# Cross-attention on one core: the scores of two slots formed together, in six PSUM banks

## Chip, core and metric

One NeuronCore of a Trainium2 chip runs the whole kernel in one launch. The metric is device time in microseconds (us). Below, PE is TensorE (matmuls), DVE is VectorE, ACT is ScalarE, POOL is GpSimd and SP is the queue that issues most DMAs. PSUM has eight banks of 512 fp32 per partition; matmuls write there, and SBUF is the working memory.

## What is computed

```python
a = layer_norm(audio_kv, gamma, beta)                      # 32 x 375 x 512
Q = heads(x @ Wq.T); K = heads(a @ Wk.T); V = heads(a @ Wv.T)   # 16 heads of 32
scores = einsum('bhtd,bhsd->bhts', Q, K) / sqrt(32)        # 112 queries x 375 keys
attn = softmax(where(mask, scores, -inf))
out = (attn @ V) @ Wo.T
return x + tanh(gate) * out                                # 32 x 112 x 512, all fp32
```

The large products are taken in three passes of a split (high part times high part, high times low, low times high), so one product over 512 inputs is 12 matmuls.

## The kernel before

The batch of 32 is cut into 128 **slots**: a slot is one batch with one group of four heads, so a batch has four. Keys run in three chunks of 125. The layer norm is folded in: the scores are made from raw context, and each chunk is scaled by the rows' `rstd` when ACT evicts it.

A slot `n` goes through these steps, each on one engine, handed on by semaphores:

- PE projects K (`project_k`, product at L874, bank `KB`), ACT copies it to `kT` (L654).
- PE forms the scores (`scores`, L1023): 12 matmuls of 32 rows, four heads on the four 32-row strips of the array, into the four banks of `sbank` (24 instructions in the trace). ACT evicts three chunks of 125x448 (`scores_out`, L574) into `prob`, which has four slots (`NB`).
- DVE takes maxima in each quadrant of 32 (`quadrant_maxima`, L780). SP stores them to DRAM and loads them back in another order (`exchange_maxima`, L332, L339). DVE reduces them (`row_maximum`, L767) and spreads them to 128x448 by a transpose (L770) into `spread`.
- DVE subtracts `spread` from the three chunks (`subtract_maximum`, L790); ACT takes the exponentials (L635).
- POOL adds the three chunks (`sum_chunks`, L451 and L455); PE forms the weighted sums (L1042) and the denominators (L1054) for two slots at a time in bank `PB`; ACT copies them out (L613).

Once per batch, PE projects V three times and the output once (L874, bank `VO`), ACT evicts them (L663, L590), DVE takes row statistics (L704, L707), normalises (`normalise`, L795 to L805, which uses `spread` for the denominators) and forms the low half of the split (`low_half`, L809). POOL finishes `rstd` (`row_statistics`, L393 to L402), makes the low half of the context (`context_lo`, L424, once per slot), adds the bias to x (`add_bias`, L436) and the output (`result`, L442).

The order on each engine is written out by hand, unrolled: the function `slot` of each engine lists what it does in slot `n`, most of it for slots `n-1` (evictions), `n-3` (subtraction, exponential) and `n-4` (weighted sums). PE, in a pair of slots, has: K, V, [weighted sums of two slots], scores, K, V or output, scores. The eight banks are: four for scores, `KB` = 4, `VO` = 5, `MB` = 6, `PB` = 7. `spread` lies in PSUM:

```python
KB, VO, MB, PB = 4, (5, 5), 6, 7
spread = bank[MB][:, 0:HT]
```

Of the kernel before, what the change touches and what calls it, by code (L numbers as in the profile page):

```python
# [5 lines left out]
F32 = mybir.dt.float32  # L6
# [8 lines left out]
KT = D // 128  # L15
# [7 lines left out]
LOOP = 2 * KT  # L23
# [10 lines left out]
def xattn(nc, xT, x, ctx, ctxT, mask, wqT, wkT, wvT, woT, gamma, beta, gate, out, row_max):  # L34
    es = ExitStack()
    with es:
# [54 lines left out]
        def cut_f(name):  # L91
# [35 lines left out]
        rden = sb("rden", [128, BLK])  # L127

        sbank = es.enter_context(nc.psum_tensor("sbank", [128, HC, 512], F32))
        bank = [sbank[:, h, :] for h in range(HC)] + [  # L130
            es.enter_context(nc.psum_tensor(f"bank{i}", [128, 512], F32))[:, :] for i in range(4, 8)]
# [5 lines left out]
        mean_bank = {"k": bank[3], "v": bank[7]}  # L137
        bv_bank, bo_bank = bank[6][:, 0:KT], bank[7]
# [52 lines left out]
        s_mm = sem("s_mm")  # L191
        s_out = sem("s_out")
# [25 lines left out]
        passed = sem("passed")  # L218
# [9 lines left out]
        def live(i, k, shift, count):  # L228
            return not isinstance(i, int) or 0 <= k * i + shift < count

        def behind(i, k, shift):
            return not isinstance(i, int) or k * i + shift > 0

        def first_two(i, c):
            return isinstance(i, int) and 2 * i + c < 2

        def wait_apart(engine, s, value):
            engine.wait_ge(s, value)
            if not isinstance(value, int):
                engine.sem_inc(passed)  # L240

        def slots(engine, slot, first=-1, last=SLOTS // LOOP + 2):
            for i in range(first, last):
                for r in range(LOOP):
                    slot(i, r)

        def v_item(r):
            b, u = r // KT, r % KT
            return {3: (b + 1, 0), 0: (b, 1), 1: (b, 2), 2: (b, None)}[u]

        def late_v(i, c, j):

            return isinstance(i, int) and 2 * i + c == B - 1 and j > 0

        def is_slot(i, r, n):
            return isinstance(i, int) and LOOP * i + r == n

        def weighted(n):

            if n >= SLOTS - 1:  # L260
                return [n - 3] if n - 3 < SLOTS else []
            return [n - 4, n - 3] if n % 2 == 0 and n >= KT else []

        def whole(i, c):

            return live(i, 2, c, B) and not (isinstance(i, int) and 2 * i + c == B - 1)
# [4 lines left out]
        def load_ctx(queue, i, m):  # L271

            if behind(i, LOOP, m - 2 * KT + 1):
                wait_apart(queue, c_done, i * LOOP + (m - 2 * KT + 1))
            queue.dma_start(cn[:, m % (2 * KT), :], ctxT_v[i * 2 + m // KT, :, m % KT, :]) \
                .then_inc(ld_ctx[m % (2 * KT)], 16)

        def load_rows(queue, i, c):
            if behind(i, 2, c):
                wait_apart(queue, stats_done, i * 2 + c)  # L280
            for part in (slice(0, 120), slice(120, SP_)):
                queue.dma_start(rows[part, :, :], rows_v[i * 2 + c, part, :, :]).then_inc(ld_rows, 16)

        @block.sync
        def _(sync):
            def load_xT(i, g):
                sync.dma_start(xraw[:, g, :, :], xT_v[:, :, bass.ds(i * (2 * GN) + g * GN, GN)]) \
                    .then_inc(ld_xT[g], 16)
# [4 lines left out]
            def load_x(i, c):  # L293
                sync.dma_start(xy[0:T, c % 2, :], x[i * 2 + c, :, :]).then_inc(ld_x[c % 2], 16)
# [6 lines left out]
            load_xT(0, 1)  # L301
            load_rows(sync, 0, 0)
            load_w("k", raw_k)
            sync.wait_ge(xr_done, 1)
            load_xT(1, 0)
            load_w("v", raw_v)
            sync.wait_ge(xr_done, 2)
            load_xT(1, 1)
            load_w("o", raw_o)
            load_rows(sync, 0, 1)  # L310
            for m in range(KT):
                load_ctx(sync, 0, m)
            for n in range(4, GROUPS):
                sync.wait_ge(xr_done, n - 1)
                load_xT(n // 2, n % 2)
            sync.dma_start(mask_u8[0:B, :], mask).then_inc(ld_mask, 16)
            load_rows(sync, 0, 2)
            for m in range(KT, 2 * KT):
                load_ctx(sync, 0, m)
            sync.wait_ge(mean_mm["v"], 1)  # L320
            load_x(0, 0)
            sync.wait_ge(bv_mm, 1)
            load_x(0, 1)

            def exchange_maxima(i, r):

                p = LOOP * i + r - 1
# [3 lines left out]
                sync.wait_ge(quad_max, i * LOOP + r)  # L331
# [4 lines left out]
                wait_apart(sync, max_stored, i * (16 * LOOP) + r * 16)  # L336
# [6 lines left out]
            def slot(i, r):  # L343
                c, u = divmod(r, KT)
                if live(i, LOOP, r - 1, SLOTS):
                    exchange_maxima(i, r)
                if u == 0:
                    if live(i, 2, c - 3, B):
                        wait_apart(sync, y_done, i * 2 + (c - 2))
                        sync.dma_start(out[i * 2 + (c - 3), :, :], xy[0:T, (c - 3) % 2, :]) \  # L350
                            .then_inc(stored[(c - 3) % 2], 16)
                if u == 1 and live(i, 2, c - 1, B) and not first_two(i, c - 1):
                    wait_apart(sync, stored[(c - 1) % 2], i * 16 + (c - 1) // 2 * 16)
                    load_x(i, c - 1)
            slots(sync, slot)
# [4 lines left out]
        def _(pool):  # L360
# [22 lines left out]
            def then(ins):  # L383
                ins.then_inc(ln_step, 1)
                steps[0] = steps[0] + 1
                wait_apart(pool, ln_step, steps[0])

            def row_statistics(i, c):

                P = SP_  # L390
                steps[0] = i * (2 * STEPS) + c * STEPS
                wait_apart(pool, stats_done, i * 2 + (c + 1))
# [5 lines left out]
                if not first_two(i, c):  # L398

                    wait_apart(pool, s_out, i * (LOOP * ST) + (c - 1) * KT * ST)  # L400
                    wait_apart(pool, v_done, i * (2 * ST) + (c - 1) * ST)
# [16 lines left out]
            def context_lo(i, r, ahead):  # L418
                if not live(i, LOOP, r + ahead, SLOTS):
                    return  # L420
                m = r + ahead
                p, k = m // KT % 2, m % KT
                wait_apart(pool, c_hi, i * LOOP + (m + 1 - KT))
# [4 lines left out]
            def wait_x(i, c):  # L428
                if c % 2:
                    wait_apart(pool, ld_x[1], (i + (c + 1) // 2) * 16)  # L430
                else:
                    wait_apart(pool, ld_x[0], (i + c // 2 + 1) * 16)

            def add_bias(i, c):
                wait_x(i, c)
# [3 lines left out]
            def result(i, c):  # L439
                wait_apart(pool, xb_done, i * 2 + (c + 1))  # L440
                wait_apart(pool, y_out, i * 2 + (c + 1))
# [3 lines left out]
            def sum_chunks(i, r):  # L445

                q, h = (r - 3) % NB, (r - 3) % 2
                wait_apart(pool, exp_done, i * (LOOP * ST) + ((r - 3) * ST + 2))
                if behind(i, LOOP, r - 4):
                    wait_apart(pool, pv_mm, i * LOOP + (r - 4))  # L450
                pool.tensor_tensor(psum[0:SP_, h, :], prob[0:SP_, q, 0, :], prob[0:SP_, q, 1, :],  # L451
                                   ALU.add).then_inc(sum_half, 1)
                wait_apart(pool, sum_half, i * LOOP + (r - 2))
                wait_apart(pool, exp_done, i * (LOOP * ST) + ((r - 3) * ST + 3))
# [3 lines left out]
            def slot(i, r):  # L458
                c, u = divmod(r, KT)
                if is_slot(i, r, 0):  # L460
                    mask_bias()
                if behind(i, LOOP, r + 2):
                    context_lo(i, r, 5)
                if u == 1 and live(i, 2, c + 1, B) and not first_two(i, c + 1):
                    row_statistics(i, c + 1)
                if live(i, LOOP, r - 3, SLOTS - 3):
                    sum_chunks(i, r)
                if u == 0 and whole(i, c - 2):
                    add_bias(i, c - 2)
                if is_slot(i, r, SLOTS + 3):  # L470
                    add_bias(i, c - 1)
                if u == 3 and whole(i, c - 2):
                    result(i, c - 2)
# [4 lines left out]
            row_statistics(0, 0)  # L478
# [5 lines left out]
            row_statistics(0, 1)  # L484
# [14 lines left out]
            slots(pool, slot)  # L499

        @block.scalar
        def _(act):
# [14 lines left out]
            def q_group(n):  # L517
                for m in range(KT):
                    act.wait_ge(q_mm, n * KT + m + 1)
                    act.activation(qT[:, n * GB:n * GB + GB, m, :], bank[KT * (n % 2) + m][:, 0:GN]  # L520
                                   .rearrange("p (b t) -> p b t", t=T), ACT.Copy).then_inc(q_out, 1)

            def context_hi(i, r):
                m = r + 6
                c, k = divmod(m, KT)
                act.wait_ge(ld_ctx[m % (2 * KT)], (i + m // (2 * KT) + 1) * 16)
# [601 lines left out]
```

## Time and profile before

| | |
|---|---|
| three runs | 977.51, 980.29, 980.42 us; median 980.29 us |
| profiled execution | span 975.2 us from the first to the last instruction; its own time outside the span is not on the page, so the median stands 5.1 us above the span |
| granted PE clock, mean | 0.998 |
| busy | PE 98%, PE weight loads 83%, DVE 82%, ACT 71%, POOL 60% of the span |

The first 95 us or so project Q and prepare the weights; the last 25 us or so finish the last slots. Between lies a stretch that repeats every batch. [...]

### The profile page before, as it was taken

Reading aid. Unit: us, or ns where it says so; the run is one execution under the profiler, and the core shown is the slowest. Engines: PE = TensorE matmul, PEld = TensorE weight load, DVE = VectorE, ACT = ScalarE, POOL = GpSimd, SP = SyncE. Lnnn points to the kernel's source line nnn. Section 1 sums busy time; section 2 is a strip of 40 time slices with the busy share of each in tenths; the row PEclk is TensorE's granted clock in tenths of the full one; section 3 lists DMA queues with packets and bytes.
Section 4 is the critical chain, followed back from the end, with each engine's and each line's share of the span. In section 5 each row is a group of like instructions: output and inputs, shape, how many; then the busy total and the mean of one; then the engine's idle time right before and its main releaser. Section 6 shows DMA issues by size and latency. Waiting matters only on the chain.

```text
span 975.2 us, 26736 instructions
## 1 busy us (share of the span) xinstructions
PE 954.5 (98%) x10703; PEld 805.6 (83%) x10703; DVE 795.5 (82%) x1446; ACT 694.3 (71%) x1301; POOL 588.6 (60%) x661
## 2 busy tenths in 40 slices
PE   8999999999999999999999999999999999999976
PEld 7889878888888888888888888888888888888864
DVE  6962588888888888888988888888888888888786
ACT  2422677778777787777877777777778777787773
POOL 0851356676666666666767666666676666666641
PEclk9999999999999999999999999999999999999999
DMA  9750333433333343333333333343332334331111
GB/s 280 224 148 24 74 82 79 101 90 80 85 88 94 87 101 94 98 98 92 87 79 86 99 88 94 93 100 99 96 93 72 83 96 95 87 100 39 34 38 48
DMA packets 80093, 90.89 MB, mean 93 GB/s; under 512 B 21888, under 2 KB 58752, under 8 KB 79968
## 3 DMA queue, kind: packets, MB, share of 16 engines
q10 hardware_dynamic: 29311, 46.24, 19.4%
q1 hardware_dynamic: 50657, 42.93, 16.5%
q8 instruction: 85, 1.39, 0.6%
q14 instruction: 40, 0.33, 0.1%
HBM read 79.05 MB, written 10.09 MB: 91 GB/s over the span
## 4 chain that ended last, share of the span: by engine, by line
PE 91%; DMA 3%; DVE 2%; POOL 2%; ACT 1%; issue 0%; SPq 0%; ACTq 0%; DVEq 0%; POOLq 0%
PE bank L874 64%; PE sbank L1023 11%; PE bank L1042 8%; PE bank L897 3%; PE bank L1054 2%; PE sbank L897 2%; DMA qT<-in_wvT 1%; ACT shared_f L574 1%; POOL gbo L411 1%; DVE shared_f L790 1%; POOL xy L415 1%; DMA row_stats<-rmax 1%; ACT shared_f L635 0%; DMA qT<-in_wqT 0%; POOL shared_f L451 0%
## 5 line engine op out<-in xcount | busy, mean ns | idle before, releaser
L574 ACT ACTIVATE shared_f<-sbank,maskT,rstd 125x448 f32<-125x448 f32 x384 | 250.5, 722 | 128.0 <-PE sbank L1023 128.0
L451 POOL TENSOR_TENSOR shared_f<-shared_f 125x448 f32<-125x448 f32 x125 | 146.9, 1175 | 276.7 <-ACT shared_f L635 276.7
L874 PE MATMUL bank<-shared_r,w_k 128*128 128x376 f32 x1536 | 298.0, 343 | 1.2 <-ACT shared_f L654 1.2
L780 DVE TRANSPOSE_TENSOR_REDUCE rmax<-shared_f 128x14 f32<-128x448 f32 x384 | 220.5, 620 | 89.3 <-ACT shared_f L574 82.5
L874 PE MATMUL bank<-w_v,shared_r 128*125 128x512 f32 x1152 | 284.9, 396 | 0.0
L874 PEld LDWEIGHTS bank<-shared_r,w_k 128*128 128x128 f32 x1536 | 258.2, 188 | 14.9 <-ACT shared_f L654 1.4
L874 PEld LDWEIGHTS bank<-w_v,shared_r 128*125 128x125 f32 x1152 | 213.5, 186 | 45.5
L790 DVE TENSOR_TENSOR shared_f<-shared_f,bank 125x448 f32<-125x448 f32 x384 | 215.4, 616 | 4.4
L635 ACT ACTIVATE shared_f<-shared_f 125x448 f32<-125x448 f32 x384 | 198.0, 579 | 6.6 <-DVE shared_f L790 6.6
L455 POOL TENSOR_TENSOR shared_f<-shared_f 125x448 f32<-125x448 f32 x125 | 143.6, 1149 | 9.8
L1023 PEld LDWEIGHTS sbank<-qT,shared_f 32*125 32x125 f32 x3072 | 95.3, 183 | 36.9 <-issue 36.9
L1023 PE MATMUL sbank<-qT,shared_f 32*125 32x112 f32 x3072 | 118.1, 282 | 2.2 <-ACT shared_f L574 2.2
L424 POOL TENSOR_TENSOR shared_r<-cn,shared_r 128x375 fp32r<-128x375 f32 x124 | 114.1, 921 | 9.6 <-ACT shared_r L530 9.5
L1042 PEld LDWEIGHTS bank<-shared_f 125*32 125x32 f32 x3072 | 71.3, 110 | 30.4 <-issue 24.4
L1042 PE MATMUL bank<-shared_f 125*32 125x112 f32 x3072 | 87.7, 261 | 5.4 <-ACT shared_f L613 3.4
L663 ACT ACTIVATE shared_f<-bank,rstd 125x512 f32<-125x512 f32 x94 | 64.6, 687 | 39.7 <-PE bank L874 39.7
L874 PE MATMUL bank<-w_o,shared_r 128*112 128x512 f32 x372 | 91.6, 394 | 0.1
L770 DVE STREAM_TRANSPOSE bank<-top 128x448 f32<-128x448 f32 x128 | 84.4, 660 | 4.4
L874 PEld LDWEIGHTS bank<-w_o,shared_r 128*112 128x112 f32 x372 | 64.5, 174 | 18.3 <-DVE shared_r L809 0.3
L654 ACT ACTIVATE shared_f<-bank 128x376 f32<-128x376 f32 x128 | 61.9, 484 | 8.6 <-issue 5.5
L530 ACT ACTIVATE shared_r<-cn 128x375 fp32r<-128x375 f32 x124 | 64.8, 523 | 0.3 <-issue 0.3
L704 DVE BATCH_NORM_STATS2 stats<-rows 125x6 f32<-125x512 f32 x96 | 58.9, 667 | 0.8 <-DMA rows<-in_ctx 0.8
(95 smaller groups left out, 775.9 us busy)
## 6 DMA issues: line engine op xcount, KB each, us to landing
cn<-in_ctxT ACTq DMA_DIRECT2D x120, 187.5 KB, 2.5
rows<-in_ctx ACTq DMA_DIRECT2D x29, 720.0 KB
xy<-in_x SPq DMA_DIRECT2D x32, 224.0 KB, 3.4
out<-xy SPq DMA_DIRECT2D x32, 224.0 KB, 3.6
shared_f<-in_xT SPq DMA_DIRECT2D x7, 896.0 KB, 9.2
x<-row_stats SPq DMA_DIRECT2D x64, 84.0 KB
x_odd<-row_stats SPq DMA_DIRECT2D x64, 84.0 KB
row_stats<-rmax SPq DMA_DIRECT2D x128, 21.0 KB
```

The source lines that it names most:

```text
L424: pool.tensor_tensor(cT[:, p, 1, k, 0:S], cn[:, m % (2 * KT), :], cT[:, p, 0, k, 0:S].bitcast(F32), ALU.subtract) \
L451: pool.tensor_tensor(psum[0:SP_, h, :], prob[0:SP_, q, 0, :], prob[0:SP_, q, 1, :], ALU.add).then_inc(sum_half, 1)
L455: pool.tensor_tensor(psum[0:SP_, h, :], psum[0:SP_, h, :], prob[0:SP_, q, 2, :], ALU.add).then_inc(sum_done, 1)
L530: act.activation(cT[:, c % 2, 0, k, 0:S], cn[:, m % (2 * KT), :], ACT.Copy) \
L574: act.activation(prob[0:SP_, (r - 1) % NB, j, :].rearrange("p (h t) -> p h t", h=HC), sbank[0:SP_, :, T * j:T * j + T], ACT.Identity, bias ...
L635: act.activation(prob[0:SP_, (r - 3) % NB, j, :], prob[0:SP_, (r - 3) % NB, j, :], ACT.Exp, scale=SCALE).then_inc(exp_done, 1)
L770: dve.transpose(spread.rearrange("p (k a) -> p k a", a=32), top[:, :].unsqueeze(2).to_broadcast([128, BLK, 32])) \
L780: last = dve.tensor_reduce(rmax[:, (r - 1) % 2, BLK * j:BLK * j + BLK], prob[:, (r - 1) % NB, j, :].rearrange("p (k a) -> p k a", a=32), A ...
L790: dve.tensor_tensor(prob[0:SP_, (r - 3) % NB, j, :], prob[0:SP_, (r - 3) % NB, j, :], spread[0:SP_, :], ALU.subtract).then_inc(sub_done, 1)
L874: last = pe.matmul(dst, l, m, start=(start and k == 0), stop=(stop and k == len(pairs) - 1))
L1023: last = pe.matmul(bank[h][0:SP_, T * j:T * j + T], kT[part, r % 2, SP_ * j:SP_ * j + SP_], qT[part, 2 * i + c, u, :], start=True, stop=True)
L1042: pe.matmul(bank[PB][HD * h:HD * h + HD, p % 2 * T:p % 2 * T + T], v_sb[0:SP_, c % 2, j, col:col + HD], prob[0:SP_, p % NB, j, T * h:T * h ...
```

## The change

PE, ACT, DVE, POOL and SP are written for pairs of slots (64 of them). PE does K of slot 2m, V, K of slot 2m+1, V or output, the weighted sums of the pair before the last, and then the scores of both slots in one stretch. The scores of two slots (six chunks of four heads) take six banks, two of which hold a third chunk each. The weighted sums go to the bank of K. `spread` gets a tensor in SBUF. ACT evicts the six chunks, one K, then takes the exponential of slot 2m-1; the exponential of slot 2m comes at the end of its pair.

```diff
-        KB, VO, MB, PB = 4, (5, 5), 6, 7
-        spread = bank[MB][:, 0:HT]
-        late_bank = {1: bank[VO[0]], 2: bank[KB]}
+        spread = sb("spread", [128, HT])
+        psum_all = es.enter_context(nc.psum_tensor("banks", [128, 8, 512], F32))
+        bank = [psum_all[:, i, :] for i in range(8)]
+        KB, VO = 6, 7
...
+        def score_place(n, j):
+            r = 3 * (n % 2) + j
+            if r < 2:
+                return (0, 1, 2, 3), (r, r, r, r)
+            if r < 4:
+                return (0, 1, 4, 5), (r, r, r - 2, r - 2)
+            return (2, 3, 4, 5), (r - 2, r - 2, r - 2, r - 2)
...
 (PE)
+            def scores(n):
+                c, u = divmod(n, KT)
+                pe.wait_ge(k_done, n + 1)
+                if n % 2 == 0:
+                    need(pe, s_out, n * ST)
                 for j in range(ST):
+                    banks, places = score_place(n, j)
+                    if n % 2 and j == 1:
+                        pe.wait_ge(s_row, n // 2 + 1)
                     for h in range(HC):
...
+                    if n % 2 == 0 and j == 1:
+                        last.then_inc(s_row, 1)
+                if n % 2:
+                    last.then_inc(s_mm, 1)
...
+            def slot_pair(m):
+                c, odd = divmod(m, 2)
+                project_k(2 * m)
+                if not odd:
+                    project_v(c, 0)
+                elif c < B - 1:
+                    project_v(c, 2)
...
+                project_k(2 * m + 1)
+                if not odd and c < B - 1:
+                    project_v(c, 1)
+                if odd and 2 <= c < B - 1:
+                    output(c - 2, c * ST + ST)
+                if pair(m - 2):
+                    pe.wait_ge(k_done, 2 * m + 2)
+                    weighted_sums(2 * m - 4, bank[KB])
...
+                scores(2 * m)
+                scores(2 * m + 1)
...
 (ACT)
+            def slot_pair(m):
+                c, odd = divmod(m, 2)
+                if pair(m):
+                    second_out(m)
+                if pair(m - 2):
+                    weighted_out(2 * m - 4)
+                if pair(m):
+                    scores_out(2 * m)
+                    scores_out(2 * m + 1)
+                if pair(m + 1):
+                    k_out(2 * m + 2)
+                if pair(m - 1):
+                    exponential(2 * m - 1)
...
+                if pair(m + 1):
+                    first_out(m + 1)
...
+                for n in (2 * m + 6, 2 * m + 7):
+                    if n < SLOTS:
+                        context_hi(n)
+                if pair(m + 1):
+                    k_out(2 * m + 3)
+                    if odd and whole(c - 1):
+                        high_half(c - 1)
+                if pair(m) and m < PAIRS - 1:
+                    exponential(2 * m)
...
 (DVE)
+            def slot_pair(m):
+                c, odd = divmod(m, 2)
+                if pair(m - 1):
+                    row_maximum(2 * m - 1)
+                    subtract_maximum(2 * m - 1)
+                if not odd and whole(c - 2):
+                    low_half(c - 2)
+                quadrant_maxima(2 * m)
+                quadrant_maxima(2 * m + 1)
+                if not odd and 2 <= c + 2 < B:
+                    statistics(c + 2)
+                if odd and whole(c - 1):
+                    normalise(c - 1)
+                if m < PAIRS - 1:
+                    row_maximum(2 * m)
+                    subtract_maximum(2 * m)
...
 (POOL)
+            def slot_pair(m):
+                c, odd = divmod(m, 2)
...
+                if pair(m - 1):
+                    sum_chunks(2 * m - 2)
+                    sum_chunks(2 * m - 1)
+                if not odd and m >= 0:
+                    if c + 1 < B and c > 0:
+                        row_statistics(c + 1)
+                    if whole(c - 2):
+                        add_bias(c - 2)
+                if odd and whole(c - 2):
+                    result(c - 2)
+                for n in (2 * m + 6, 2 * m + 7):
+                    if n < SLOTS:
+                        context_lo(n)
...
 (SP)
+            for m in range(PAIRS):
+                c, odd = divmod(m, 2)
+                exchange_maxima(2 * m)
+                exchange_maxima(2 * m + 1)
+                if not odd and c > 2:
+                    store(c - 3)
+                if odd and c > 2:
+                    load_x(c - 1)
```

The instructions of the subtraction, the reductions, the exponentials and the sums keep their shapes. Banks used while the kernel starts and while it ends are renumbered, and the end takes its last four slots as one pair and two single ones.

## Rows read from the trace of the kernel before

**Rows 1.** Page, busy time of each engine (busy us, share, instructions).
```profile
PE 954.5 (98%) x10703; PEld 805.6 (83%) x10703; DVE 795.5 (82%) x1446; ACT 694.3 (71%) x1301; POOL 588.6 (60%) x661
```

**Rows 2.** Page, the chain that ended last, share of the span by engine.
```profile
PE 91%; DMA 3%; DVE 2%; POOL 2%; ACT 1%; issue 0%; SPq 0%; ACTq 0%; DVEq 0%; POOLq 0%
```

**Rows 3.** Windows: one batch; length, busy time and instructions by engine.
```profile
500.00:526.96 26.96, 26.96 (x321) 22.69 (x320) 23.07 (x44) 20.82 (x39) 17.56 (x21) 1.00 0.38 92
```

**Rows 4.** Timeline of PE: start, duration, line, output and inputs, count.
```profile
502.56 2.33 PE L874 MATMUL bank<-shared_r,w_k 128*128 128x376 f32 x12
504.73 2.95 PE L874 MATMUL bank<-w_v,shared_r 128*125 128x512 f32 x12
...
506.58 1.10 PE L874 MATMUL bank<-w_v,shared_r 128*125 128x512 f32 x4
507.61 0.92 PE L1023 MATMUL sbank<-qT,shared_f 32*125 32x112 f32 x24
508.14 0.40 PE L1023 MATMUL sbank<-qT,shared_f 32*125 32x112 f32 x8
508.25 0.29 PE L1023 MATMUL sbank<-qT,shared_f 32*125 32x112 f32 x4
508.46 0.44 PE L874 MATMUL bank<-shared_r,w_k 128*128 128x376 f32 x1
...
513.51 1.36 PE L1042 MATMUL bank<-shared_f 125*32 125x112 f32 x48
...
526.99 1.36 PE L1042 MATMUL bank<-shared_f 125*32 125x112 f32 x48
```

**Rows 5.** Page, costliest groups: the K projections (busy, mean ns of one).
```profile
L874 PE MATMUL bank<-shared_r,w_k 128*128 128x376 f32 x1536 | 298.0, 343 | 1.2 <-ACT shared_f L654 1.2
```

**Rows 6.** By line: DVE's two-input instructions, ns min/median/max, first and last start.
```profile
L790 DVE TENSOR_TENSOR shared_f<-shared_f,bank x384: 611/614/623, 112.6 to 964.9; 125x448 f32<-125x448 f32 x192
...
L805 DVE TENSOR_TENSOR shared_f<-shared_f,bank x31: 620/620/622, 144.4 to 950.5; 128x448 f32<-128x448 f32 x31
...
L809 DVE TENSOR_TENSOR shared_r<-shared_f,shared_r x31: 624/1514/1536, 149.3 to 956.6; 128x448 fp32r<-128x448 f32 x31
```

**Rows 7.** Timeline of DVE in the same batch.
```profile
499.62 1.52 DVE L809 TENSOR_TENSOR shared_r<-shared_f,shared_r 128x448 fp32r<-128x448 f32 x1
...
502.23 1.68 DVE L790 TENSOR_TENSOR shared_f<-shared_f,bank 125x448 f32<-125x448 f32 x3
503.83 1.69 DVE L780 TRANSPOSE_TENSOR_REDUCE rmax<-shared_f 128x14 f32<-128x448 f32 x3
```

**Rows 8.** Timeline of POOL in the same batch.
```profile
499.51 1.15 POOL L455 TENSOR_TENSOR shared_f<-shared_f 125x448 f32<-125x448 f32 x1
500.62 1.66 POOL L436 TENSOR_TENSOR xy<-xy,gbo 112x512 f32<-112x512 f32 x1
...
508.01 0.98 POOL L424 TENSOR_TENSOR shared_r<-cn,shared_r 128x375 fp32r<-128x375 f32 x1
...
521.49 1.29 POOL L442 TENSOR_TENSOR xy<-xy,gated 112x512 f32<-112x512 f32 x1
```

**Rows 9.** Timeline while weights are prepared: DVE and POOL side by side.
```profile
46.11 0.69 DVE L713 TENSOR_TENSOR w_v<-qT,w_v 128x512 fp32r<-128x512 f32 x1
47.74 2.39 DVE L713 TENSOR_TENSOR w_v<-qT,w_v 128x512 fp32r<-128x512 f32 x2
...
44.59 3.57 POOL L411 TENSOR_SCALAR gbo<-qT,bv 128x512 f32<-128x512 f32 x1
48.23 1.34 POOL L415 TENSOR_TENSOR gated<-gated,gbo 128x512 f32<-128x512 f32 x1
```

**Rows 10.** Timeline of ACT: three score evictions, one of K.
```profile
502.70 1.96 ACT L574 ACTIVATE shared_f<-sbank,maskT,rstd 125x448 f32<-125x448 f32 x3 [1.87 <-PE sbank L1023]
...
506.37 0.49 ACT L654 ACTIVATE shared_f<-bank 128x376 f32<-128x376 f32 x1
```

**Rows 11.** Waits: who waited for whom, us in total, times, longest.
```profile
POOL shared_f L451 <- ACT shared_f L635: 276.7, 123, 5.5
```

More of the change, by code:

```diff
@@ L226, in xattn @@
         wT = {"k": wkT, "v": wvT, "o": woT}
[L228 to L266, printed above, removed]
+        def need(engine, s, value):
+            if value > 0:
+                engine.wait_ge(s, value)
+        def q_bank(g, m):
+            return bank[KT + (m + 2) % KT] if g else bank[m]
+        def score_place(n, j):
[5 more added lines that the diff above has]
+            return (2, 3, 4, 5), (r - 2, r - 2, r - 2, r - 2)
@@ L341, in exchange_maxima @@
                     ap=[[0, HC], [HC * ST * BLK, 32], [1, HC * ST * BLK]])).then_inc(ld_max[q], 16)
[L343 to L355, printed above, removed]
+            for m in range(PAIRS):
[6 more added lines that the diff above has]
+                    load_x(c - 1)
+            for b in range(B - 3, B):
+                store(b)
+                if b + 2 < B:
+                    load_x(b + 2)
             sync.wait_ge(stored[0], 16 * (B // 2))
@@ L456, in sum_chunks @@
                                    ALU.add).then_inc(sum_done, 1)
-            def slot(i, r):
-                c, u = divmod(r, KT)
-                if is_slot(i, r, 0):
+            def slot_pair(m):
+                c, odd = divmod(m, 2)
+                if m == 0:
                     mask_bias()
[L462 to L473, printed above, removed]
+                if pair(m - 1):
[11 more added lines that the diff above has]
+                        context_lo(n)
@@ L498, in _ @@
             pool.wait_ge(c_done, KT)
-            slots(pool, slot)
+            for m in range(-1, PAIRS):
+                slot_pair(m)
+            add_bias(B - 2)
+            result(B - 2)
+            add_bias(B - 1)
         @block.scalar
@@ new lines, in scores, with weighted @@
+                        last = pe.matmul(bank[banks[h]][0:SP_, T * places[h]:T * places[h] + T],
+                                         kT[part, n % 2, SP_ * j:SP_ * j + SP_],
+                                         qT[part, c, u, :], start=True, stop=True)
+                    if n % 2 == 0 and j == 1:
+                        last.then_inc(s_row, 1)
+                if n % 2:
+                    last.then_inc(s_mm, 1)
+            def weighted(p, j, dst):
+                c, u = divmod(p, KT)
+                for h in range(HC):
+                    col = HD * (HC * u + h)
+                    pe.matmul(dst[HD * h:HD * h + HD, :], v_sb[0:SP_, c % 2, j, col:col + HD],
+                              prob[0:SP_, p % NB, j, T * h:T * h + T],
+                              start=(j == 0), stop=(j == ST - 1))
```

560 lines of the change are left out of this document (249 added, 311 removed).

## Prediction

> **What bounds the kernel now.** I read the busy times first, then the chain, then one batch of the repeating stretch. PE is busy 98% of the span, DVE 82%, POOL 60% [rows 1]; the chain that ended last runs through PE for 91% [rows 2]. In the batch from 500.00 to 526.96 PE is busy 26.96 of 26.96 us, DVE 23.07, ACT 20.82, POOL 17.56 [rows 3]. So in that stretch every other engine is hidden, DVE with the least room: 3.9 us a batch. PE's timeline gives the period of a pair of slots: 526.99 - 513.51 = 13.48 us [rows 4]. The same timeline shows what going into and out of the scores costs, and the lines of DVE and POOL show what DVE's room depends on.
>
> **What PE saves.** Of two score stretches per pair one disappears as a stretch of its own. Going in: V's matmuls start every 0.231 us ((506.58 - 504.73) / 8), but from the fourth last to the first score it is 1.03 us, where four take 0.93: 0.10 us. The stretch: 508.46 - 507.61 = 0.85 us for six groups of four matmuls that follow each other at 508.25 - 508.14 = 0.11 us, so 0.66 would do: 0.19 us. Going out: the first K matmul lasts 0.44 us where the mean is 0.343: 0.10 us [rows 4, 5]. Together 0.39, say 0.40 us a pair, and over 64 pairs 25.6 us. PE's period would be 13.08 us a pair, 26.16 a batch.
>
> **Waits added on PE.** The odd slot's second chunk waits for the even slot's second chunk (`s_row`). Behind it stand the last eight score matmuls, then K. Two chunks, four groups at 0.11 us, lie between, 0.44 us against the 0.29 us of a group [rows 4]: I take 0. If the wait emptied the array each time, it would cost what leaving and entering costs, 0.40 us a pair, and the whole saving; a gain is excluded, since nothing is removed. The second K waits for the K copy behind six evictions: PE has a K and a V to do first, 507.61 - 502.56 = 5.05 us; ACT needs 0.14 us to start (502.70 after 502.56), twice 1.96, and 0.49: 4.55 us [rows 4, 10]. Hidden, with 0.5 us of room; if ACT comes to the evictions more than that late, PE stands, and with it the V and the weighted sums queued behind. The weighted sums share the bank of K; ACT copies them out while PE forms the scores, and PE's K waits behind that copy. The first slot's scores are evicted only when both are formed, up to 0.85 us later; DVE's reductions start later by that, with nothing added to DVE's own work. Renumbered banks at start and end, and stores and loads moved between SP's two exchanges of a pair: I take 0; SP's exchange for a second slot queues behind the first, and DVE has statistics or a normalisation to do meanwhile. Shapes of evictions and exponentials stay; six banks instead of four give the same 448 columns, so 0, either way by less than the 0.5 us of room.
>
> **What the new place of `spread` costs.** This is the term that decides. Today the subtraction reads `prob` from SBUF and `spread` from PSUM: 384 of them take 611 to 623 ns, whatever POOL does, and so does the normalising product (620 to 622). The low half, of the same 448 columns but with both inputs in SBUF, takes 624 ns at the least and 1514 in the median [rows 6]. One instance shows why: it starts at 499.62 while POOL's sum runs from 499.51 to 500.66, and ends at 501.14; had it run its 0.624 us undisturbed at the end, it began at 500.52, when POOL was nearly done. POOL's next instruction starts at 500.62 and takes 1.66 us, but ends 1.14 us after DVE's [rows 7, 8]. So the two engines take turns: a two-input DVE instruction from SBUF and a POOL addition do not run together. After the change all 12 subtractions of a batch and the normalising product are of that kind, besides the low half: 14 instead of 1.
>
> Without any of these waits DVE needs 23.07 - 0.89 = 22.2 us a batch [rows 3, 6]. PE's new period is 26.16. So DVE can wait 4.0 us a batch, 0.28 us for each of the 14, before it becomes the bound, and 4.8 us, 0.34 each, before the change loses to the old period; and that is if it never idles for anything else.
>
> How many waits are there? The order of the new program says which POOL instructions are ready when. POOL's idle time is nearly all waiting for exponentials (276.7 us before its first sum) [rows 11], so its work comes in bunches behind them. In a pair, ACT's exponential of slot 2m-1 comes after the six evictions and a K, about when DVE finishes the reductions. POOL then adds that slot's chunks (two instructions of 1.15 us) while DVE does statistics or normalises, some 2 us. When DVE comes to the subtractions of slot 2m, POOL has three instructions queued: the bias (1.14) or the result (1.29), and two context halves (0.85 to 0.98) [rows 8]. If the engines alternate, three subtractions meet three of them: 0.9 + 0.85 + 0.85 = 2.6 us. The subtractions of slot 2m+1 follow at once, and POOL's sums of slot 2m, whose exponentials have just been taken, run beside them: one whole wait of about 1.0 and part of another, 1.4 us together. That is 4.0 us a pair, 8.0 a batch, 0.67 us for each of the 12. The lower bound is 0 (POOL always elsewhere; a gain is excluded, as 614 ns in PSUM stands against 624 in SBUF at the least). The upper is the low half's 0.89 for all 14, 12.5 us. I take 8.0, nearer to the low half, the only row of this kind in this stretch.
>
> DVE then needs 22.2 + 8.0 = 30.2 us a batch, 3.24 over today's 26.96. Over 31 batches (the first and last are incomplete) that is +100 us. PE's 25.6 us are not to be had, since PE waits for DVE by way of ACT: late subtractions delay the exponential, the evictions behind it, and the K copy. The span goes from 975.2 to 1075.6; with the 5.1 us by which the median of the runs stands above the span, 1080.7, say **1080 us**.
>
> The start of the kernel shows the same turns, and an exception [rows 9]. Two back-to-back two-input instructions from 47.74 take 2.39 us, where one undisturbed takes 0.69: POOL's addition, begun at 48.23 during the first, came in between them. But at 46.11 such an instruction ran in 0.69 us although a POOL instruction had stood since 44.59 behind the DVE instruction before it: DVE passed it.
> [...]
>
> **Rivals.**
> 1. *DVE keeps its turn through three subtractions.* Then each group waits at most once. Four groups at about 0.6 us on average (POOL is busy 17.56 of 26.96 us [rows 3], a wait is at most 0.9), and 0.5 each for product and low half: 3.4 us, so DVE needs 25.6 us, below 26.16. PE stays the bound and keeps its saving: 980.3 - 25.6 = 955 us, up to 970 if some waits reach PE. For it: the row at 46.11. Against it: 47.74, and that POOL's L455 and L436, issued back to back, let the low half in between [rows 8, 9]. Faster; chance 0.21.
> 2. *Full waits everywhere.* 22.2 + 12.5 = 34.7 us, +7.7 a batch, +240: 1220 us. For it: the low half's median is near its maximum [rows 6]. Against it: POOL would need 14 large instructions lined up with 14 of DVE's, and as the period grows POOL idles more. From 1150 on: chance 0.08.
> 3. *Waits that nearly cancel the saving.* About 4.8 us of DVE waits a batch, or the `s_row` wait emptying the array each time at 0.40 us a pair, gives back the 25.6: 977 to 983 us. Chance 0.06.
> 4. *Milder turns*: 5 to 6 us a batch, up to 983 to 1020 us: the random meeting of the two engines rather than bunches. Chance 0.09.
>
> **How the numbers follow.** Forecast 1080, own range 1020 to 1150, chance 0.56. About 0.3% (3 us) is what a measurement of this kernel tells from no change. Slower: 0.56 + 0.08 + 0.09 = 0.73; same 0.06; faster 0.21. Cases of both signs lie far apart; the range from 956 to 1150 takes in most of the first rival, and leaves out its lowest part and the second.
>
> **What would show it.** Right: L790 of 384 instructions at a mean of about 1.2 to 1.3 us instead of 0.615, the normalising product above 0.62; DVE busy above 95% of the repeating stretch, PE well under 90%, with its idle time before K, released by ACT's K copy; a batch of about 30 us. PE's own saving still visible: 12 groups of scores in one stretch of about 1.5 us. Wrong: subtractions near 0.62 to 0.8 us and a batch near 26.2 us (first rival); subtractions undisturbed and PE idle before the odd slot's second chunk (`s_row`); or DVE idle while PE waits, by the maxima exchange through DRAM, which I left out of the sum.

## The result: 24% slower

The changed kernel takes 1214.18 us in the median of 4 runs (1209.93 to 1218.74), against 978.9 us of the kernel before in the same comparison: a ratio of 1.2407, 95% interval 1.237 to 1.2444. The direction was forecast, the size was not: 1080 us, with a range that ended at 1150.

The page of the kernel after, busy times and the chain that ended last by engine and by line, answers to [rows 1, 2]; its line numbers have moved by a few.

```profile
PE 1005.3 (83%) x10687; PEld 873.3 (72%) x10687; DVE 835.7 (69%) x1446; ACT 694.1 (57%) x1299; POOL 602.6 (50%) x663
...
DMA 59%; DVE 24%; issue 7%; PE 5%; SPq 3%; POOL 1%; ACT 0%; ACTq 0%; DVEq 0%; POOLq 0%
DMA row_stats<-rmax 39%; DMA x_odd<-row_stats 17%; DVE shared_f L793 9%; DVE rmax L783 7%; PE banks L905 4%; DVE spread L774 4%; SPq L335 3%; DVE top L771 3%; DMA x<-row_stats 1%; DMA qT<-in_wvT 1%; PE banks L882 1%; POOL gbo L406 1%; POOL xy L410 0%; DVE shared_r L812 0%; DMA qT<-in_wqT 0%
```

No engine is near full. The chain has left PE and lies in two small DMAs, the store and the load of the maxima. One batch, from one block of weighted sums to the one two pairs on, as a window (length, then busy time by engine), answers to [rows 3]: 34.13 us instead of 26.96.

```profile
601.18:635.31 34.13, 27.80 (x321) 24.22 (x320) 23.64 (x43) 20.85 (x39) 17.92 (x21) 0.95 0.27 73
```

DVE's busy time in this batch grew by only 0.6 us, to 23.64; over the run it grew by 40.2 us (795.5 to 835.7), 1.3 a batch. Forecast were 30.2 us a batch. DVE waits instead. Its timeline in one pair (idle time before an instruction and what ended it stand in brackets):

```profile
608.34 3.27 DVE L783 TRANSPOSE_TENSOR_REDUCE rmax<-shared_f 128x14 f32<-128x448 f32 x6
...
613.12 0.81 DVE L808 TENSOR_TENSOR shared_f<-shared_f,spread 128x448 f32<-128x448 f32 x1
619.29 0.43 DVE L771 TENSOR_REDUCE top<-x 128x14 f32<-128x168 f32 x1 [5.36 <-DMA x<-row_stats]
619.76 0.65 DVE L774 STREAM_TRANSPOSE spread<-top 128x448 f32<-128x448 f32 x1
620.44 1.70 DVE L793 TENSOR_TENSOR shared_f<-shared_f,spread 125x448 f32<-125x448 f32 x3
623.10 0.44 DVE L771 TENSOR_REDUCE top<-x_odd 128x14 f32<-128x168 f32 x1 [0.97 <-DMA x_odd<-row_stats]
623.58 0.65 DVE L774 STREAM_TRANSPOSE spread<-top 128x448 f32<-128x448 f32 x1
624.26 1.95 DVE L793 TENSOR_TENSOR shared_f<-shared_f,spread 125x448 f32<-125x448 f32 x3
...
626.67 3.27 DVE L783 TRANSPOSE_TENSOR_REDUCE rmax<-shared_f 128x14 f32<-128x448 f32 x6
```

The same time on SP's queue, issue of store (L328) and load (L335); a load is issued when its store has landed (by the waits, L335 stood for the stores 128 times, 416.0 us in all):

```profile
610.11 0.52 SPq L328 DMA_DIRECT2D row_stats<-rmax  x1
615.72 0.54 SPq L335 DMA_DIRECT2D x<-row_stats  x1
616.35 0.53 SPq L328 DMA_DIRECT2D row_stats<-rmax  x1
619.75 0.53 SPq L335 DMA_DIRECT2D x_odd<-row_stats  x1
...
628.43 0.52 SPq L328 DMA_DIRECT2D row_stats<-rmax  x1
631.26 0.54 SPq L335 DMA_DIRECT2D x<-row_stats  x1
```

This is a closed loop. DVE reduces slot 2m; here the store takes 5.6 us (from its issue to that of the load), the load 3.6 (to the row maximum), and DVE stands from 613.93 to 619.29 before that slot's row maximum. Behind it in DVE's queue are two subtractions, and only behind those the reductions of the next pair, whose maxima are then stored: 628.43 - 610.11 = 18.3 us for this pair, where PE needs 13.1. In all DVE stands 320 us before row maxima, most of it for the even slot's (us in total, times, longest):

```profile
DVE top L771 <- DMA x<-row_stats: 270.5, 64, 8.7
...
DVE top L771 <- DMA x_odd<-row_stats: 49.9, 59, 1.5
```

The slow store is not new. In the kernel before, SP shows the same length, 5.8 us, behind row loads that ACT issued at 510.77 and 511.40; it is hidden because DVE came to that row maximum only at 522.18, without idle time before it:

```profile
510.77 0.60 ACTq L282 DMA_DIRECT2D rows<-in_ctx  x1
...
512.03 0.54 SPq L332 DMA_DIRECT2D row_stats<-rmax  x1
517.79 0.54 SPq L339 DMA_DIRECT2D x_odd<-row_stats  x1
...
522.18 0.45 DVE L767 TENSOR_REDUCE top<-x_odd 128x14 f32<-128x168 f32 x1
```

### The profile page after: what moved, and what is told of

It is laid out like the page before. It is cut to its first block, busy times and chain, and to the rows that moved or that the text cites. A ratio compares the mean times of both kernels' runs of the same rounds, so it can differ in the third digit from the quotient of the medians.

```text
span 1216.9 us, 26606 instructions
## 1 busy us (share of the span) xinstructions
PE 1005.3 (83%) x10687; PEld 873.3 (72%) x10687; DVE 835.7 (69%) x1446; ACT 694.1 (57%) x1299; POOL 602.6 (50%) x663
## 4 chain that ended last, share of the span: by engine, by line
DMA 59%; DVE 24%; issue 7%; PE 5%; SPq 3%; POOL 1%; ACT 0%; ACTq 0%; DVEq 0%; POOLq 0%
DMA row_stats<-rmax 39%; DMA x_odd<-row_stats 17%; DVE shared_f L793 9%; DVE rmax L783 7%; PE banks L905 4%; DVE spread L774 4%; SPq L335 3%; DVE top L771 3%; DMA x<-row_stats 1%; DMA qT<-in_wvT 1%; PE banks L882 1%; POOL gbo L406 1%; POOL xy L410 0%; DVE shared_r L812 0%; DMA qT<-in_wqT 0%
## 5 line engine op out<-in xcount | busy, mean ns | idle before, releaser
L882 PE MATMUL banks<-shared_r,w_k 128*128 128x376 f32 x1536 | 347.8, 385 | 192.8 <-ACT shared_f L613 189.3
L882 PEld LDWEIGHTS banks<-shared_r,w_k 128*128 128x128 f32 x1536 | 315.8, 224 | 208.5 <-issue 198.3
L882 PE MATMUL banks<-w_v,shared_r 128*125 128x512 f32 x1152 | 297.7, 409 | 0.0
L793 DVE TENSOR_TENSOR shared_f<-shared_f,spread 125x448 f32<-125x448 f32 x384 | 274.6, 768 | 4.4
L882 PEld LDWEIGHTS banks<-w_v,shared_r 128*125 128x125 f32 x1152 | 227.2, 198 | 48.7
L563 ACT ACTIVATE shared_f<-banks,maskT,rstd 125x448 f32<-125x448 f32 x384 | 243.7, 742 | 0.8 <-PE banks L1022 0.8
L771 DVE TENSOR_REDUCE top<-x 128x14 f32<-128x168 f32 x64 | 28.5, 445 | 270.5 <-DMA x<-row_stats 270.5
L1022 PE MATMUL banks<-qT,shared_f 32*125 32x112 f32 x3072 | 100.9, 275 | 0.0
L1022 PEld LDWEIGHTS banks<-qT,shared_f 32*125 32x125 f32 x3072 | 89.5, 183 | 11.3 <-issue 11.3
L882 PE MATMUL banks<-w_o,shared_r 128*112 128x512 f32 x372 | 93.9, 402 | 3.0 <-DVE shared_r L812 3.0
L1035 PE MATMUL banks<-shared_f 125*32 125x112 f32 x3072 | 87.9, 261 | 7.7 <-ACT shared_f L572 3.1
## 6 DMA issues: line engine op xcount, KB each, us to landing
cn<-in_ctxT ACTq DMA_DIRECT2D x120, 187.5 KB, 2.5
```

Of the source, the lines that this page charges most:

```text
L563: act.activation(prob[0:SP_, n % NB, j, :] .rearrange("p (a h t) -> p a h t", a=2, h=2), score_view(n, j), ACT.Identity, bias=maskT[0:SP_, ...
L793: dve.tensor_tensor(prob[0:SP_, p % NB, j, :], prob[0:SP_, p % NB, j, :], spread[0:SP_, :], ALU.subtract).then_inc(sub_done, 1)
L882: last = pe.matmul(dst, l, m, start=(start and k == 0), stop=(stop and k == len(pairs) - 1))
L1022: last = pe.matmul(bank[banks[h]][0:SP_, T * places[h]:T * places[h] + T], kT[part, n % 2, SP_ * j:SP_ * j + SP_], qT[part, c, u, :], star ...
L1035: pe.matmul(dst[HD * h:HD * h + HD, :], v_sb[0:SP_, c % 2, j, col:col + HD], prob[0:SP_, p % NB, j, T * h:T * h + T], start=(j == 0), stop ...
```

## Experiments

Each ran beside the kernel before (976.8 to 980.1 us); times are medians. "After" stands for the kernel after the change. A `...` in a diff or a view marks lines left out, within a line what is left out of it.

**No exchange.** After, with the store and the load left out from the third slot on.
```diff
                 q = p % 2
                 if p > 1:
-                    sync.wait_ge(ld_max[q], p // 2 * 16)
+                    return
...
-                dve.wait_ge(ld_max[p % 2], (p // 2 + 1) * 16)
+                dve.wait_ge(ld_max[p % 2], 16)
```


> The kernel after without the exchange of the maxima through DRAM from the third slot on: every later slot subtracts maxima of the first two slots (that part of the computation is left out); all work on DVE, ACT, POOL and PE stays. Theory A: the loop's 59% of DMA goes, DVE or PE bounds, 990 to 1080 us. Theory B: 1180 us or more.

1007.62 us (ratio to before 1.0305, 1.0283 to 1.0326). So 1214.2 - 1007.6 = 206 us come with the exchange. What is left is DVE: 394 of 400 us busy, with subtractions at a mean of 1016 ns (windows; then the group by line: busy, mean ns).
```profile
500.00:900.00 400.00, 375.03 (x4612) 323.55 (x4611) 394.14 (x611) 297.62 (x557) 279.36 (x289) 1.00 0.27 72
...
L791 DVE TENSOR_TENSOR shared_f<-shared_f,spread 125x448 f32<-125x448 f32 x384 | 369.7, 1016 | 4.4
```

**No exchange, no sums on POOL.** PE forms the denominators from the three chunks.
```diff
-                    sum_chunks(2 * m - 2)
-                    sum_chunks(2 * m - 1)
...
-                    denominator(psum[:, q, :], to[:, (2 + q) * T:(3 + q) * T], True, True) \
+                    for j in range(ST):
+                        last = denominator(prob[:, (p + q) % NB, j, :], ..., j == 0, j == ST - 1)
```


> The same without the exchange, and with PE forming the denominators from the three chunks so that POOL has no sums (as in e4). What the turns between DVE and POOL cost once the exchange is out of the way: theory A 30 us or less below e7, theory B 100 us or more below e7. PE has 1 us a pair more to do, so not under 980 us.

994.51 us, 13 below the run before it; but PE is 98% busy with the longer denominators, so this is only a lower bound on what the turns cost.

**PE's saving alone.** The same with denominators of the usual length, from constants.
```diff
-                    for j in range(ST):
-                        last = denominator(prob[:, (p + q) % NB, j, :], ..., j == 0, j == ST - 1)
+                    denominator(psum[:, q, :], ..., True, True).then_inc(pv_mm, 1)
```


> The kernel after with the exchange from the third slot on and POOL's sums both left out, and the denominators formed from constants (maxima, sums and denominators are so left out of the computation), in the same number of matmuls as after the change. Nothing but PE's own order should bound it. The forecast's first term (0.40 us a pair saved by one score stretch instead of two): 950 to 962 us. If the one stretch saved nothing: 975 us or more.

950.34 us against 976.84: 26.5 us, where the forecast had 25.6. In the window from 500 to 900 PE is busy 400.00 of 400.00 us, and a batch takes 26.17 us (weighted sums at 505.56 and 531.73), where the forecast had 26.16:
```profile
505.56 1.36 PE L1031 MATMUL banks<-shared_f 125*32 125x112 f32 x48
...
531.73 1.36 PE L1031 MATMUL banks<-shared_f 125*32 125x112 f32 x48
```
From here to the 1007.6 above, 57 us go to POOL's sums and the turns they take. The subtractions still meet POOL's other work here, at a mean of 887 ns, but DVE stays hidden behind PE.

**`spread` in SBUF in the kernel before.**
```diff
-        spread = bank[MB][:, 0:HT]
+        spread = sb("spread", [128, HT])[:, :]
```


> The kernel before with one line changed: spread lies in SBUF, as after the change; order and banks stay. [...] Theory B (the forecast: DVE and POOL taking turns is what costs the time): 5 to 8 us a batch, 1020 to 1100 us.

995.55 us, 1.0155 (1.0109 to 1.0201): 15.6 us more. That is below the range of theory B, and 5.6 us above the 975 to 990 us of the other theory, in which the loop through the exchange costs the time and the lengthened subtractions fit into DVE's room. The subtractions' mean rises from 616 to 754 ns. DVE's busy time grows by 83 us (795.5 to 878.8), so most of it fits into DVE's room. The middle hardly moves (median 618 ns), single ones reach 1686 (by line: min/median/max):
```profile
L790 DVE TENSOR_TENSOR shared_f<-shared_f,spread x384: 609/618/1686, 113.6 to 978.7; 125x448 f32<-125x448 f32 x192
```

**After without POOL's sums**, exchange in place (the edit of the second run alone).

> The kernel after, with POOL's sums of the three chunks taken out: PE forms the denominators from the three chunks itself, some 1 us more a pair on PE, which idles 4 us there. The subtractions then meet hardly any POOL work. Theory A: only the lengthening of the six subtractions of a pair on the chain goes, at most 0.15 us each, 0.9 us a pair: 1150 to 1190 us. Theory B: the time falls to 1000 us or less.

1203.22 us: 11 us gained, less than either theory had. DVE's busy time falls by 41 us (835.7 to 794.6), but its stands before the odd slot's maxima grow by 26 (49.9 to 76.1): while DVE has to stand for the exchange, most of what a shorter subtraction saves is waited out again. The reverse, `spread` back in PSUM after the change, wasn't tried: in every pair PE and ACT use all eight banks that the kernel declares.

**Loads later.** ACT issues the loads of context and rows at the end of its pair.
```diff
-                for n in range(2 * m + 11 - (m < 0), 2 * m + 13):
...
                 if pair(m) and m < PAIRS - 1:
                     exponential(2 * m)
+                for n in range(2 * m + 11 - (m < 0), 2 * m + 13):
+                    if n < SLOTS:
+                        load_ctx(act, n)
+                if odd and 3 <= c + 3 < B:
+                    load_rows(act, c + 3)
```


> The kernel after, with ACT issuing the loads of context and rows at the end of its pair, behind the exponential of slot 2m, instead of just before the maxima are stored. Theory A: the store of the maxima, 2.8 to 5.6 us from its issue to the load's issue now, comes back to some 2.2 us; in all 3 to 4 us less a batch, 1090 to 1130 us. Theory B: no change, 1205 to 1220 us.

1138.97 us: 75 us gained, a little short of the expectation. In the kernel after the change, ACT had issued these loads right before the store of 610.11 (each row load 720 KB, a context load 187.5 KB):
```profile
608.46 0.82 ACTq L267 DMA_DIRECT2D cn<-in_ctxT  x2
...
609.32 0.45 ACTq L273 DMA_DIRECT2D rows<-in_ctx  x1
```
With the loads later the first stores of two pairs take 2.39 and 2.12 us:
```profile
602.87 0.52 SPq L328 DMA_DIRECT2D row_stats<-rmax  x1
605.26 0.54 SPq L335 DMA_DIRECT2D x<-row_stats  x1
...
619.03 0.52 SPq L328 DMA_DIRECT2D row_stats<-rmax  x1
621.15 0.54 SPq L335 DMA_DIRECT2D x<-row_stats  x1
```
DVE's stands before row maxima fall by 185 us, from 320.4 to 135.2 (113.7 and 21.5). But as DVE stands less it meets POOL more: the subtractions' mean rises from 768 to 1005 ns, and DVE's busy time by 94 us (835.7 to 929.8). That is why no more than 75 us are left.
```profile
DVE top L771 <- DMA x<-row_stats: 113.7, 62, 4.1
...
L793 DVE TENSOR_TENSOR shared_f<-shared_f,spread 125x448 f32<-125x448 f32 x384 | 366.1, 1005 | 4.4
```

**The exponential of slot 2m late, alone.**
```diff
                 if pair(m - 1):
+                    exponential(2 * m - 2)
                     exponential(2 * m - 1)
...
-                if pair(m) and m < PAIRS - 1:
-                    exponential(2 * m)
```


> The kernel after, with on ACT alone the exponential of slot 2m moved behind the evictions of the next pair. Theory A: DVE never waits for evictions there, it stands before the row maxima, so PE's waits shrink but the period stays: 1195 to 1220 us. The forecast's way (late subtractions hold the exponential, the evictions and so the reductions): 1150 us or less.

1187.99 us, 26 gained: nearly the expectation for the loop (1195 to 1220). DVE still stands before the row maxima (223 and 71 us), so ACT's order was not what closed the loop.

**DVE interleaved.**
```diff
+                quadrant_maxima(2 * m)
                 if pair(m - 1):
                     row_maximum(2 * m - 1)
                     subtract_maximum(2 * m - 1)
                 if not odd and whole(c - 2):
                     low_half(c - 2)
-                quadrant_maxima(2 * m)
                 quadrant_maxima(2 * m + 1)
```


> The kernel after, with DVE's order alone changed: the reductions of slot 2m come before the row maximum and subtraction of slot 2m-1, those of slot 2m+1 behind them. Each slot's maxima then have 6 us more or so of DVE work between being stored and being wanted. Theory A: DVE no longer stands before the row maxima, the period falls from 34 us a batch to 26.2 to 28, 955 to 1010 us. Theory B: the turns with POOL stay or grow, so 1150 us or more.

1130.39 us: 84 gained, between the two expectations. The exchange has shrunk to 10% of the chain (DMA), but a second loop stands in its place, and it is the one that the forecast had described: the subtraction of slot 2m, lengthened by turns, holds the exponential, which stands ahead of the evictions that DVE waits for (172.8 us in all).
```profile
617.81 4.25 DVE L793 TENSOR_TENSOR shared_f<-shared_f,spread 125x448 f32<-125x448 f32 x3
624.40 1.81 DVE L783 TRANSPOSE_TENSOR_REDUCE rmax<-shared_f 128x14 f32<-128x448 f32 x3 [2.34 <-ACT shared_f L563]
```

**DVE interleaved and loads later** (both edits).

> The kernel with DVE interleaved (1130 us), with the loads of context and rows behind the exponential of slot 2m, as in the run that gained 75 us on the kernel after. Theory A: that gain came by way of the maxima's exchange, which here is mostly hidden behind DVE's work, so little is left of it: 1110 to 1130 us. If the loads had gained by something else than the exchange (ACT's queue, the context's own arrival), the gain would come again: 1070 us or less.

1179.1 us: 49 slower than interleaved alone, a miss. The gain of 75 us is not there again, but in the new place the loads' issue stands on ACT ahead of the evictions (ACTq is 5% of the chain). The cause is read from the chain; no run holds it apart:
```profile
633.05 2.47 ACTq L273 DMA_DIRECT2D rows<-in_ctx  x2
635.57 0.69 ACT L583 ACTIVATE shared_f<-banks,rstd 125x512 f32<-125x512 f32 x1 [2.81 <-issue]
```

**Interleaved, exponentials late, loads behind the second K copy** (the edits above together, the loads moved once more).

> The kernel with DVE interleaved, and on ACT both exponentials behind the evictions of the next pair (the one of slot 2m no longer stands ahead of the evictions of 2m+2), and the loads of context and rows behind the second K copy. Theory A (a loop through the DRAM exchange, and a second one through the exponential of slot 2m ahead of the evictions): DVE's 173 us of waiting for evictions in the interleaved kernel mostly go, 985 to 1040 us. [...]

1115.73 us, a miss of theory A; it fits the 1080 us or more of the theory that the turns set DVE's time. But the trace names another cause than the turns, which the next run tests: both exponentials come later, POOL's sums with them, and the context halves behind the sums hold PE's K (waits):
```profile
PE banks L881 <- POOL shared_r L416: 76.8, 30, 2.8
```

**Context halves first on POOL**, on top of that.
```diff
                     sum_chunks(2 * m - 1)
+                for n in (2 * m + 6, 2 * m + 7):
+                    if n < SLOTS:
+                        context_lo(n)
...
                     result(c - 2)
-                for n in (2 * m + 6, 2 * m + 7):
-                    if n < SLOTS:
-                        context_lo(n)
```


> The kernel with DVE interleaved and both exponentials late (1116 us), with POOL's order alone changed: the two context halves of a pair come before the row statistics, bias and result instead of behind them. In the 1116 us PE stood 77 us before K, released by a context half. Theory A (once the exchange is off the path, each further wait is one of order, and the turns with POOL set a floor near the 1008 us of the kernel without exchange): 1020 to 1060 us. Theory B (the turns alone hold the 1116 us): no change, 1105 us or more.

1014.22 us, 102 gained, more than expected: it was POOL's order that held the 1116 us. Turns are to be seen in its timelines of DVE and POOL: three subtractions in 4.18 us, against 1.70 undisturbed, beside three POOL instructions.
```profile
603.93 4.18 DVE L792 TENSOR_TENSOR shared_f<-shared_f,spread 125x448 f32<-125x448 f32 x3
...
603.83 2.19 POOL L416 TENSOR_TENSOR shared_r<-cn,shared_r 128x375 fp32r<-128x375 f32 x2
605.98 1.65 POOL L428 TENSOR_TENSOR xy<-xy,gated 112x512 f32<-112x512 f32 x1
```

**The same without POOL's sums**, denominators from one chunk.

> The reordered kernel (1014 us: DVE interleaved, exponentials late, context halves first) without POOL's sums, the denominators taken from the first chunk alone (two thirds of the denominator are left out), exchange in place. If the turns between DVE and POOL hold the 1014 us: 955 to 985 us. If what is left is order (both slots' evictions behind one wait, weighted sums and K in one bank): 1000 us or more.

1007.4 us: 7 gained, so order held it, not the turns. PE stands before its second product of V or output, for ACT's copy of the first V, which waits behind both exponentials:
```profile
606.58 3.01 PE L878 MATMUL banks<-w_o,shared_r 128*112 128x512 f32 x12 [0.66 <-ACT shared_f L580]
```

**V between the exponentials**, and the low half earlier.
```diff
                     exponential(2 * m - 2)
+                if pair(m + 1):
+                    first_out(m + 1)
+                if pair(m - 1):
                     exponential(2 * m - 1)
...
+                if not odd and whole(c - 2):
+                    low_half(c - 2)
                 if pair(m - 1):
                     row_maximum(2 * m - 1)
```


> The reordered kernel (1014 us) with two moves: ACT evicts the first V between the two exponentials instead of behind both (PE stood there 0.6 us a pair), and DVE makes the low half before the subtraction of slot 2m-1 (PE's output product stood for it 1 us a batch). If order is what holds the 1014 us: 960 to 990 us, where DVE, busy 26.2 us of a 28 us batch with its turns, takes over as the bound. If the turns hold it already: 1005 us or more.

974.19 us against 980.11, ratio 0.9939 (0.9925 to 0.9953): a gain of 0.6% on the kernel before, small but clear of the noise. Its page and the window from 500 to 900 show DVE at its limit, with subtractions at a mean of 970 ns. So it's probably the turns that now hold back most of PE's 26 us; this order without POOL's sums wasn't run.
```profile
DVE 68%; PE 18%; issue 7%; DMA 4%; ACT 1%; POOL 1%; ACTq 0%; DVEq 0%; SPq 0%; POOLq 0%
...
500.00:900.00 400.00, 391.94 (x4795) 338.87 (x4794) 393.58 (x644) 306.86 (x584) 297.94 (x299) 1.00 0.37 92
```

## Why the prediction was wrong

- **PE's saving: right.** 0.40 us a pair was forecast, 25.6 us; 26.5 us came out where nothing else bounds. The scores of a pair are one stretch of 1.58 us, and no wait for `s_row` is seen.
- **The step that failed** is the one that took 0 for SP: "SP's exchange for a second slot queues behind the first, and DVE has statistics or a normalisation to do meanwhile." I compared the two in words, not in numbers. Meanwhile is some 2 us of statistics and 1.6 of the second slot's reductions; the exchange, in the lines above, is 2.1 to 5.6 us of store and 3.6 of load. It was the first slot's exchange that DVE stood for, not the second's that the sentence speaks of (270.5 against 49.9 us). In the kernel before, DVE's order put another slot's subtraction and reductions, and here the normalisation, between a slot's reductions and its row maximum (512.03 to 522.18, 10 us); in the new order the row maximum of slot 2m comes before any reduction of the next pair. The trace of the kernel before had it: I had read neither the store's time on SP nor the time to the row maximum. The price is 206 us. The prediction did name DVE idle by the exchange as a sign of being wrong, and that sign is what came.
- **The turns with POOL: seen, but smaller.** Forecast 8.0 us a batch, with a POOL instruction between any two subtractions wherever POOL has work. That was the author's estimate, and no run shows it as a rule: three subtractions took 4.18 us in the lines above in one place, 1.70 in another. In the kernel after it is 12 times (0.768 - 0.616), 1.8 us, in part since POOL's work falls into the time DVE stands; with the exchange left out 12 times (1.016 - 0.616), 4.8, and 0.9 more for the normalising product, 1520 ns there: 5.7 together. Left alone they would have made 1007.6 us, not 1080: I lined up more POOL instructions with the subtractions than meet them on average. That is the fourth rival, milder turns (5 to 6 us a batch, up to 1020 us), which had a chance of 0.09. The low half, on which the forecast modelled the subtractions, lost its own wait: 1484 ns in the mean before, 616 after, and 1577 in the run with the context halves first. So the wait of such an instruction can't be carried from one order to another. It went by what POOL had to do when DVE came to it: in the kernel before a sum of POOL ran beside the low half of 499.62 [rows 7, 8], in the kernel after POOL's last instruction had ended at 624.65 when the low half began at 626.13 (0.61 us).
```profile
L793 DVE TENSOR_TENSOR shared_f<-shared_f,spread 125x448 f32<-125x448 f32 x384 | 274.6, 768 | 4.4
L793 DVE TENSOR_TENSOR shared_f<-shared_f,spread x384: 609/620/1691, 113.2 to 1204.7; 125x448 f32<-125x448 f32 x192
...
L812 DVE TENSOR_TENSOR shared_r<-shared_f,shared_r 128x448 fp32r<-128x448 f32 x31 | 19.1, 616 | 0.6 <-ACT shared_r L589 0.6
```
- **The path to PE** was only partly as told. PE stands before K, but for ACT's copy of the weighted sums (L613, 189 us), in ACT's queue behind the exponential of slot 2m, not for the K copy. In the repeating stretch DVE never waited for evictions (one wait of 19.0 us stands at the start); that loop appeared only once DVE was interleaved.
- **The rivals.** The nearest to the measured time, full waits at 1220 us, was right by accident: the subtractions' median is 620 ns. The first rival, that three subtractions pass as a block, falls by the 4.18 us above: 2.48 more than undisturbed, longer than any one POOL instruction beside them took (two together 2.19, the third 1.65). There they alternate; they don't always do so one for one. With the exchange left out, one subtraction took 2.45 us, 1.83 more than the median of 0.62 in the kernel after, beside two context halves of 1.77 us together that began after it:
```profile
614.97 2.45 DVE L791 TENSOR_TENSOR shared_f<-shared_f,spread 125x448 f32<-125x448 f32 x1
...
615.16 1.77 POOL L414 TENSOR_TENSOR shared_r<-cn,shared_r 128x375 fp32r<-128x375 f32 x2
```
The forecast's reading, that the engines alternate, doesn't give the order of these last lines; what decides it stays open, and so does why the two hold each other up: the traces show the lengthened times alone.

The sum of what was measured: 978.9 before, less 26.5 for PE's stretch, gives about 952 (measured 950.3); with POOL's sums and their turns 1007.6; with the exchange in the loop 1214.2. The last two steps do not simply add: with the exchange in place, taking POOL's sums away gains 11 us, not 57.

## What to carry to other kernels

When work is regrouped, write for each round trip through another queue how much of the waiting engine's own work lies between sending and wanting, before and after, and set it beside the trip's measured time. A written order that waits for a trip ahead of the work that starts the next trip has a loop. Here it took 34.1 us a batch where PE needs 26.2, and no engine looked full in it (PE's 83% was the most). Several orders then have to change together: 1214, 1130, 1116, 1014 and 974 us came from moving a few lines at a time, and each step showed the next wait.

## What the runs showed of the hardware

A store of 21 KB took 2.1 us from its issue to that of the load behind it (499.77 to 501.90 in the kernel before), and 5.6 to 5.8 us in the lines above where the two row loads of 720 KB had been issued from ACT's queue just before, in both kernels. Behind a context load alone, that of 504.11 in the kernel before, it took 2.1 us as well (505.59 to 507.71); right behind two of them, at 628.43 in the kernel after, it took 2.8 us. Issuing two row loads took ACT's queue from 0.86 us (609.32 to 610.18 in the kernel after) to 2.47 us (from 633.05, DVE interleaved and loads later), by place.

After its longer stands in this trace PE ran slower: the K product that followed 4.66 us of idle time took 3.84 us, against 2.31 after 1.67 us, at a granted clock of 0.54 against 1.00. From 150 to 641 us of the trace the 14 first K products of a pair that followed 3.46 to 6.06 us of idle time took 3.70 to 4.10 us; of the 15 that followed 0.68 to 1.85 us, 13 took 2.30 or 2.31, and two (500.77 and 640.40) 3.75 and 3.48. The mean granted clock of the run was 0.906, against 0.998 in the kernel before. DVE waited for no evictions in that stretch, so no cost is put on it.

```profile
606.10 2.31 PE L882 MATMUL banks<-shared_r,w_k 128*128 128x376 f32 x12 [1.67 <-ACT shared_f L613]
...
623.90 3.84 PE L882 MATMUL banks<-shared_r,w_k 128*128 128x376 f32 x12 [4.66 <-ACT shared_f L613]
```
Windows over the two products (length, busy time and instructions by engine; the third number from the end is the granted clock):
```profile
606.10:608.25 2.15, 2.15 (x13) 2.15 (x13) 2.12 (x4) 2.15 (x4) 0.77 (x1) 1.00 0.00 0
623.90:627.58 3.68, 3.68 (x13) 3.68 (x13) 3.65 (x7) 3.55 (x6) 0.76 (x1) 0.54 0.00 0
```
